# Writing out the counted loops of four engines in a gated cross-attention and mixture-of-experts kernel

## The chip, the core and the metric

The kernel runs on one core of a Trainium2 chip. The core has five engines that run their own instruction streams and meet only through semaphores: TensorE (PE in the profile; PEld is its weight load), VectorE (DVE), ScalarE (ACT), GpSimd (POOL) and SyncE (SP, here only DMA issues). The metric is the device time of one execution in microseconds; less is better.

## What is computed

```
x = x + tanh(g_xattn) * LN(rs * (softmax(q k^T / 4 + mask) v) Wo^T ...)   # 32 x 56 queries, 32 x 1500 context rows, 16 heads of 16
x = x + tanh(g_ffn)   * sum_e w_tok[:, e] * (relu(LN(x) w_fc[e])^2 w_proj[e])   # 8 experts, the two best of each token
```

q comes from the layer-normed x, k and v from the context (`ctx_2048`, 32 x 1500 x 256). All matrices are float32. The kernel keeps their accuracy by splitting each operand into a high and a low part and adding three products (high x high, high x low, low x high).

## The kernel before

**Attention stage.** The 32 batch entries are taken as 16 pairs (`NP`). A pair has 6 groups q of 500 context positions (`PG`), and a group 4 chunks of 125 positions, so a pair has 24 chunks c. TensorE projects k and v of the *next* group while it works on the scores of this one. Its order in a group is: `pv` of the four chunks of the group before, `kv_part(half 0, part 0)`, `scores(c)`, `kv_part(half 0, part 1)`, `scores(c+1)`, `scores(c+2)`, `kv_part(half 1, part 0)`, one of five side tasks (`beside_scores`; none in group 4), `scores(c+3)`, `kv_part(half 1, part 1)`.

Everything that leaves PSUM is shared out by hand. ScalarE takes `exps` (exp of a chunk's scores, L663), `k_hi_evac` (L649), `ctx_high` (L656) and most DMA issues. VectorE clips the probabilities (`clip`, L971), adds the bias of v (`v_evac_step`, L834), takes the low part of k (`k_lo_evac`, L819) and of the context (`ctx_low`, L825), and does the layer norms, sums and divisions in `before_clips`. GpSimd does `inv_std`, `x_plus_beta` and the low part of the expert weights (`expert_lo`).

Two rings matter here. `v_ps` is one PSUM bank: `kv_part(n, half, s, 0)` waits for `v_evac` of the half before it (L413), which VectorE does after the clip of chunk c, which waits for the exp of chunk c. And `pv` waits for `clip_done` of its chunk (L465).

**Expert stage.** 7 blocks f of 256 tokens (`NF`) by 8 experts e. In a step TensorE does `fc(f, e)` and, two steps behind, `proj(f, e - 2)`; between them lie ScalarE's relu (L770), VectorE's square (L1104), ScalarE's high part (L775) and GpSimd's low part (L354). VectorE adds the result to `acc` (L1094).

**Loops.** All the code of an engine is one Python function that calls a helper for a pair or a block. TensorE's pairs are written out already. Pairs 1 to 14 of ScalarE, VectorE and GpSimd, and blocks f from 2 (GpSimd: from 1) of the experts, stand in a `Fori`: one copy of the body with the counter in a register. There every address that depends on the pair, and every semaphore count to wait for, is computed by the engine's sequencer with register instructions (REGISTER_ALU, ISA in the listings; ALU_OP, FUSED_REGOPS, MOVE in the trace). Pair 0 and pair 15 have their constants in the instructions, as have blocks 0 and 1 of the experts. So the same work occurs in one trace in both forms. SyncE has a loop of its own for the loads of the context (L289).

Of the kernel before, what the change touches and what calls it, by code (L numbers as in the profile page):

```python
# [25 lines left out]
NP = B // 2  # L26
# [9 lines left out]
NF = TOK // FT  # L36
# [17 lines left out]
def gated_cross_attention_moe(nc, a, x1_dram, out):  # L54
# [5 lines left out]
    with ExitStack() as ctx:  # L60
# [6 lines left out]
        def plain(ap):  # L67
            return ap.bitcast(fp32)
# [6 lines left out]
        def step(f, e):  # L75

            return f * NE + e if isinstance(f, int) else None
# [231 lines left out]
        @block.gpsimd  # L309
        def _(pool):  # L310
            pool.memset(mhalf[:, :], -0.5).then_inc(ones_done, 1)
            pool.memset(vst[:, :, :, :, HD:VW], 1.0).then_inc(ones_done, 1)
            pool.wait_ge(ones_done, 2)

            def inv_std(ln, i):

                pool.wait_ge(var_done[ln], i + 1)
                pool.tensor_tensor(rstd[ln][0:PW, :], var_e[ln][0:PW, :], mhalf[0:PW, :], ALU.pow)\  # L318
                    .then_inc(rstd_done[ln], 1)

            def x_plus_beta(i):
                pool.wait_ge(xr_in, 16 * i + 16)
                pool.tensor_tensor(xr[0:PW, :], xr[0:PW, :], bet[0:PW, :], ALU.add).then_inc(xb_done, 1)

            def expert_lo(i):

                pool.wait_ge(wehi_done, i + 1)
                pool.tensor_tensor(we_lo[:, bass.ds(i, 1), :, :].squeeze(1), w_raw[:, :, :],
                                   plain(we_hi[:, bass.ds(i, 1), :, :].squeeze(1)), ALU.subtract).then_inc(welo_done, 1)

            def pair(i, first=False, final=False):

                expert_lo(i)
                if not final:
                    inv_std(0, i + 1)
                if not first:
                    x_plus_beta(i - 1)
                    inv_std(1, i - 1)
                    inv_std(2, i - 1)

            inv_std(0, 0)
            pool.wait_ge(scale_done, 4)
            pair(0, first=True)
            with pool.Fori(1, NP - 1) as i:
                pair(i)
            pair(NP - 1, final=True)

            def h_low(f):

                for e in range(NE):  # L350
                    u = f * NE + e
                    at = step(f, e)
                    pool.wait_ge(hhi_done, u + 1)
                    pool.tensor_tensor(h_lo[:, e % NB, :, :], h_sq[:, e % 2, :, :], plain(h_hi[:, e % NB, :, :]),  # L354
                                       ALU.subtract).then_inc(hlo_done, 1)
                    if at == 5:
                        x_plus_beta(NP - 1)
                        inv_std(1, NP - 1)
                    if at == 6:
                        inv_std(2, NP - 1)  # L360

            h_low(0)
            with pool.Fori(1, NF) as f:
                h_low(f)


# [1 line left out]
        def _(pe):  # L368
# [121 lines left out]
            def spread_sums(i):  # L490

                pe.wait_ge(sum_split, 4 * i + 4)
                pe.matmul(side_ps[:, 0:ST * PW], sumsel_r[:, :], sum_hi[:, :, :], start=True, stop=False)  # L493
                pe.matmul(side_ps[:, 0:ST * PW], sumsel_r[:, :], sum_lo[:, :, :], start=False, stop=True).then_inc(sum_done, 1)

            def out_proj(i):
                pe.wait_ge(packed, 16 * ST * (i + 1))
                for k in range(KD):
                    last = pe.matmul(side_ps[0:PW, 0:D], rec[:, 2 * k, :], wo[:, k, :], start=(k == 0), stop=(k == KD - 1))  # L499
                last.then_inc(op_done, 1)  # L500
# [84 lines left out]
            def fc(f, e):  # L585

                u = f * NE + e
                wait(pe, relu_done, u - 1)
                for m in range(KD):
                    ws = slice(m * P, (m + 1) * P)  # L590
                    for k in range(KD):
                        last = mm3(sc_ps[:, e % 2, m * FT:(m + 1) * FT], we_hi[:, 2 * e, k, ws], we_lo[:, 2 * e, k, ws],
                                   yT_hi[:, k, bass.ds(f * FT, FT)], yT_lo[:, k, bass.ds(f * FT, FT)], k == 0, k == KD - 1)
                last.then_inc(fc_done, 1)

            def proj(f, e):

                u = f * NE + e
                pe.wait_ge(hlo_done, u + 1)
                wait(pe, acc_done, 2 * u - 2)  # L600
                for t in range(2):
                    ts = slice(t * P, (t + 1) * P)
                    for k in range(KD):
                        last = mm3(sc_ps[:, 2 + e % 2, t * D:(t + 1) * D], h_hi[:, e % NB, k, ts], h_lo[:, e % NB, k, ts],
                                   we_hi[:, 2 * e + 1, k, :], we_lo[:, 2 * e + 1, k, :], k == 0, k == KD - 1)
                last.then_inc(y2_done, 1)

            def experts(f, first=False):
                for e in range(NE):
                    at = step(f, e)  # L610
                    if not (first and e == 0):
                        fc(f, e)
                    if at == 1:
                        pe.wait_ge(ylo_done, NP)
                        spread_sums(NP - 1)
                    if e >= 2:
                        proj(f, e - 2)
                    elif not first:
                        proj(f - 1, NE - 2 + e)
                    if at == 5:  # L620
                        out_proj(NP - 1)
                    if at == 9:
                        y_transpose(NP - 1)
                    if at == 12:
                        pe.wait_ge(ylo_done, NP + 1)
                        for t in range(RT, NT):
                            router(1, t)
# [4 lines left out]
            for d in range(GC, 0, -1):  # L632
                pv(NP - 1, PC - d)
            experts(0, first=True)
            experts(1)
            with pe.Fori(2, NF) as f:
                experts(f)
            proj(NF - 1, NE - 2)
            proj(NF - 1, NE - 1)
# [3 lines left out]
        def _(act):  # L643
# [112 lines left out]
                k_hi_evac(0, m, 0)  # L756
            act.wait_ge(m_ready, 1)
            pair(0, first=True)
            with act.Fori(1, NP - 1) as i:
                pair(i)  # L760
            pair(NP - 1, final=True)

            def hidden(f, first=False):
                for e in range(NE):
                    u = f * NE + e
                    at = step(f, e)
                    act.wait_ge(fc_done, u + 1)
                    if not (first and e < 2):
                        act.wait_ge(sq_done, u - 1)
                    act.activation(h_relu[:, e % 2, :, :], sc_ps[:, e % 2, :].rearrange("p (m n) -> p m n", m=KD),  # L770
                                   ACT.Relu).then_inc(relu_done, 1)
                    act.wait_ge(sq_done, u + 1)
                    if not (first and e < NB):
                        act.wait_ge(y2_done, u - NB + 1)
                    act.activation(h_hi[:, e % NB, :, :], h_sq[:, e % 2, :, :], ACT.Copy).then_inc(hhi_done, 1)  # L775
                    if at == 0:
                        sums_spread(NP - 1)
                    if at == 7:
                        store_x1(NP - 1)
                    if at == 9:  # L780
                        y_transposed(NP - 1)
                    if at == 15:
                        second_of_two(1)

            hidden(0, first=True)
            hidden(1)
            with act.Fori(2, NF) as f:
                hidden(f)
            act.wait_ge(x1_out, 16 * NP)

# [2 lines left out]
        def _(dve):  # L793
# [284 lines left out]
            dve.tensor_tensor(wr_2[:, :, 1, :], wr[:, :, :], plain(wr_2[:, :, 0, :]), ALU.subtract).then_inc(wr_split, 1)  # L1078
            dve.wait_ge(scale_done, 4)
            pair(0, first=True)  # L1080
            with dve.Fori(1, NP - 1) as i:
                pair(i)
            pair(NP - 1, final=True)

# [12 lines left out]
            def experts(f, first=False):  # L1097
                for e in range(NE):
                    u = f * NE + e
                    dve.wait_ge(relu_done, u + 1)  # L1100
                    if not (first and e < 2):
                        dve.wait_ge(hlo_done, u - 1)
                    r = h_relu[:, e % 2, :, :]
                    dve.tensor_tensor(h_sq[:, e % 2, :, :], r, r, ALU.mult).then_inc(sq_done, 1)  # L1104
                    if e >= 2:
                        accumulate(f, e - 2)
                    elif not first:
                        accumulate(f - 1, NE - 2 + e)
                    beside_experts(step(f, e))
# [31 lines left out]
                    dve.wait_ge(acc_in[2], 16)  # L1141

            experts(0, first=True)
            experts(1)
            with dve.Fori(2, NF) as f:
                experts(f)
            accumulate(NF - 1, NE - 2)
            accumulate(NF - 1, NE - 1)
# [48 lines left out]
```

## Time and profile before

| | us |
|---|---|
| three timed runs | 1261.64 (median), 1258.55, 1262.3 |
| the profiled execution, its own time | 1259.26 |
| its span, first to last instruction | 1257.2 |
| PE busy | 1235.6 (98%) |
| DVE busy | 920.3 (73%) |
| ACT busy | 697.3 (55%) |
| POOL busy | 171.1 (14%) |
| attention stage | about 12 to 1085 |
| expert stage | about 1085 to 1254 |

The time of the execution is its span and 2.1 us around it. Matmuls are pipelined and their ends are modelled, so a busy share of 98% on PE tells only that PE is seldom empty for long; a wait of 0.1 us ahead of a matmul is mostly swallowed by the modelled tail of the one before. Such waits show as longer distances between the starts of like matmuls.

### The profile page before, as it was taken

What the parts mean: (1) busy time and instruction counts of PE and PEld (TensorE: products, weight loads), DVE (VectorE), ACT (ScalarE), POOL (GpSimd) and SP (SyncE); (2) the same over time, 40 slices, a digit from 0 to 9 for tenths busy, and PEclk for the clock granted to TensorE, in tenths of its full rate; (3) what the DMA queues carried; (4) which work ended last, traced back from release to release, by engine and by line L of the source; (5) the groups of instructions that cost most, each with busy time, mean ns of one, the idle gap of its engine ahead of it and who ended that gap; (6) DMA issues with size and microseconds to landing.
All of it is one profiled execution on the core that took longest, in us unless ns stands there. A gap on an engine that the chain in (4) does not pass through costs nothing.

```text
span 1257.2 us, 58770 instructions
## 1 busy us (share of the span) xinstructions
PE 1235.6 (98%) x25460; PEld 1175.5 (94%) x25460; DVE 920.3 (73%) x1806; ACT 697.3 (55%) x854; POOL 171.1 (14%) x142
## 2 busy tenths in 40 slices
PE   6999999999999999999999999999999999999998
PEld 6999999999999999999999999999999999899998
DVE  6667777777777877777777777777777776687555
ACT  4565655655565656565655655665656565244443
POOL 0000101010101010010101010101010100154443
PEclk9999999999999999999999999999999999799999
DMA  4121212121212112121212121212121120020000
GB/s 159 43 76 38 71 54 71 53 68 39 69 55 69 56 41 67 53 71 54 71 37 72 53 71 54 71 38 69 53 69 56 54 67 7 18 63 10 17 8 17
DMA packets 29536, 68.65 MB, mean 55 GB/s; under 512 B 6038, under 2 KB 13459, under 8 KB 29331
## 3 DMA queue, kind: packets, MB, share of 16 engines
q1 hardware_dynamic: 20450, 54.61, 14.1%
q10 hardware_dynamic: 8880, 10.75, 2.7%
q8 instruction: 196, 3.21, 1.0%
q14 instruction: 10, 0.07, 0.0%
HBM read 60.77 MB, written 3.67 MB: 51 GB/s over the span
## 4 chain that ended last, share of the span: by engine, by line
PE 94%; issue 2%; DVE 2%; POOL 1%; DMA 0%; ACT 0%; DVEq 0%; POOLq 0%
PE v_ps L428 24%; PE k_ps L431 21%; PE sc_ps L454 21%; PE o_ps L469 12%; PE sc_ps L371 3%; PE sc_ps L372 3%; PE sc_ps L373 3%; PE k_ps L499 1%; PE k_ps L486 1%; POOL h_lo L354 1%; DVE prob L971 1%; PE k_ps L493 1%; PE k_ps L478 0%; PE k_ps L505 0%; DMA xq<-in_x 0%
## 5 line engine op out<-in xcount | busy, mean ns | idle before, releaser
L663 ACT ACTIVATE prob<-sc_ps,m_bias 125x896 f32<-125x896 f32 x384 | 377.1, 1008 | 336.4 <-PE sc_ps L454 335.1
L971 DVE TENSOR_SCALAR prob<-prob 125x896 f32<-125x896 f32 x384 | 237.3, 624 | 205.3 <-ACT prob L663 201.8
L428 PE MATMUL v_ps<-wv_hi,c_hi 64*125 64x256 f32 x1520 | 317.3, 288 | 3.7 <-DVE c_lo L825 2.6
L431 PE MATMUL k_ps<-c_hi,wk_hi 64*128 64x500 f32 x760 | 314.1, 413 | 0.0
L428 PE MATMUL v_ps<-wv_hi,c_lo 64*125 64x256 f32 x1520 | 301.1, 277 | 0.0
L428 PE MATMUL v_ps<-wv_lo,c_hi 64*125 64x256 f32 x1520 | 300.9, 278 | 0.0
L431 PE MATMUL k_ps<-c_lo,wk_hi 64*128 64x500 f32 x760 | 293.2, 386 | 0.0
L431 PE MATMUL k_ps<-c_hi,wk_lo 64*128 64x500 f32 x760 | 292.2, 384 | 0.0
L428 PEld LDWEIGHTS v_ps<-wv_hi,c_hi 64*125 64x125 f32 x1520 | 225.4, 183 | 16.9 <-DVE c_lo L825 2.8
L428 PEld LDWEIGHTS v_ps<-wv_hi,c_lo 64*125 64x125 f32 x1520 | 229.4, 183 | 0.0
L454 PE MATMUL sc_ps<-q_hi,kh 64*125 64x224 f32 x1536 | 229.0, 278 | 0.0
L428 PEld LDWEIGHTS v_ps<-wv_lo,c_hi 64*125 64x125 f32 x1520 | 228.4, 183 | 0.0
L454 PE MATMUL sc_ps<-q_lo,kh 64*125 64x224 f32 x1536 | 222.7, 270 | 0.0
L454 PE MATMUL sc_ps<-q_hi,kl 64*125 64x224 f32 x1536 | 222.4, 269 | 0.0
L454 PEld LDWEIGHTS sc_ps<-q_hi,kh 64*125 64x125 f32 x1536 | 180.1, 185 | 15.8 <-issue 10.0
L469 PE MATMUL o_ps<-prob,vst 125*17 125x56 f32 x12288 | 175.1, 213 | 3.3 <-issue 1.3
L469 PEld LDWEIGHTS o_ps<-prob,vst 125*17 125x17 f32 x12288 | 156.5, 98 | 19.8 <-issue 6.1
L649 ACT ACTIVATE kh<-k_ps,cst 128x500 fp32r<-128x500 f32 x192 | 130.3, 679 | 56.0 <-PE k_ps L431 55.6
L454 PEld LDWEIGHTS sc_ps<-q_hi,kl 64*125 64x125 f32 x1536 | 158.7, 186 | 0.1
L454 PEld LDWEIGHTS sc_ps<-q_lo,kh 64*125 64x125 f32 x1536 | 157.8, 185 | 0.0
L318 POOL TENSOR_TENSOR rstd<-var_e,mhalf 112x1 f32<-112x1 f32 x48 | 66.4, 1384 | 581.3 <-DVE var_e L809 581.3
L431 PEld LDWEIGHTS k_ps<-c_lo,wk_hi 64*128 64x128 f32 x760 | 141.6, 186 | 0.0
(141 smaller groups left out, 2143.4 us busy)
## 6 DMA issues: line engine op xcount, KB each, us to landing
raw<-in_ctxT SPq DMA_DIRECT2D x96, 500.0 KB, 3.5
w_raw<-in_we ACTq DMA_DIRECT2D x16, 256.0 KB, 5.1
xq<-in_x ACTq DMA_DIRECT2D x16, 112.0 KB, 2.0
xr<-in_x ACTq DMA_DIRECT2D x16, 112.0 KB, 4.2
x_scratch<-x ACTq DMA_DIRECT2D x16, 112.0 KB, 1.9
out_y<-acc SPq DMA_DIRECT2D x7, 256.0 KB, 2.0
acc<-x_scratch SPq DMA_DIRECT2D x1, 1280.0 KB, 7.3
rec<-rec SPq DMA_DIRECT2D x64, 14.0 KB, 2.6
```

The source lines that it names most:

```text
L318: pool.tensor_tensor(rstd[ln][0:PW, :], var_e[ln][0:PW, :], mhalf[0:PW, :], ALU.pow)\
L354: pool.tensor_tensor(h_lo[:, e % NB, :, :], h_sq[:, e % 2, :, :], plain(h_hi[:, e % NB, :, :]), ALU.subtract).then_inc(hlo_done, 1)
L371: pe.matmul(ps, w_h, m_h, start=first, stop=False)
L372: pe.matmul(ps, w_h, m_l, start=False, stop=False)
L373: return pe.matmul(ps, w_l, m_h, start=False, stop=last)
L428: v_last = pe.matmul(v_ps[0:TC, j * D:(j + 1) * D], c_s[v_rows, cs], w_m[v_rows, k, :], start=begin and j == 0, stop=end, skip_group_check ...
L431: k_last = pe.matmul(k_ps[:, half, 0:TG], w[k_rows, k, ws], c_m[k_rows, :], start=begin, stop=end)
L454: last = pe.matmul(sc_ps[0:TC, 2 * (c % 2) + r, m * HS * S:(m + 1) * HS * S], k[rows, g % 2, m, cs], q[rows, b, m, :, :], start=term == 0, ...
L469: last = pe.matmul(o_ps[q * 32:q * 32 + VW, col * S:(col + 1) * S], vst[0:TC, c // GC % 2, c % GC, h, :], prob[0:TC, c % PB, at * S:(at + ...
L649: act.activation(kh[:, s, m, :], k_ps[:, m, 0:TG], ACT.Identity, bias=bk[:, m:m + 1]).then_inc(k_hi, 1)
L663: act.activation(prob[0:TC, c % PB, :].rearrange("p (c n) -> p c n", c=2), sc_ps[0:TC, 2 * (c % 2):2 * (c % 2) + 2, 0:NH * S // 2], ACT.Ex ...
L971: dve.tensor_scalar(p, p, EXP_LO, EXP_HI, ALU.max, ALU.min).then_inc(clip_done, 1)
```

## The change

The `Fori` loops of ScalarE, VectorE, GpSimd (pairs) and of all four engines (expert blocks) become Python loops, so that each pair and block has its own instructions. The loop of SyncE stays.

```diff
@@ gpsimd
-            with pool.Fori(1, NP - 1) as i:
+            for i in range(1, NP - 1):
                 pair(i)
-            h_low(0)
-            with pool.Fori(1, NF) as f:
+            for f in range(NF):
                 h_low(f)
@@ tensor
             experts(0, first=True)
-            experts(1)
-            with pe.Fori(2, NF) as f:
+            for f in range(1, NF):
                 experts(f)
@@ scalar
-            with act.Fori(1, NP - 1) as i:
+            for i in range(1, NP - 1):
                 pair(i)
-            hidden(1)
-            with act.Fori(2, NF) as f:
+            for f in range(1, NF):
                 hidden(f)
@@ vector
-            with dve.Fori(1, NP - 1) as i:
+            for i in range(1, NP - 1):
                 pair(i)
-            experts(1)
-            with dve.Fori(2, NF) as f:
+            for f in range(1, NF):
                 experts(f)
```

No engine operation is added, removed or put in another order, and no wait is added. What goes are the register instructions and the branches. The listed instructions of the program rise from 316 to 923 on ScalarE, from 543 to 1808 on VectorE, from 59 to 146 on GpSimd and from 18478 to 19222 matmuls on TensorE (each with its weight load).

ScalarE, a looped pair, around the exps (L663 before, L661 after) and the evacuations of k (L649, L647), before:

```order
L661 REGISTER_ALU
L663 ISA [waits pv_done,scores_done]
L663 ACTIVATE prob<-sc_ps,m_bias 125x896
L646 REGISTER_ALU
L649 ACTIVATE kh<-k_ps,cst 128x500 [waits kproj_done]
L653 ISA
L73 ISA [waits raw_in0]
L656 ACTIVATE c_hi<-raw 128x1000 [waits vproj_done,kproj_done]
```

and after, the same place in pair 1:

```order
L661 ACTIVATE prob<-sc_ps,m_bias 125x896 [waits pv_done,scores_done]
L647 ACTIVATE kh<-k_ps,cst 128x500 [waits kproj_done]
L654 ACTIVATE c_hi<-raw 128x1000 [waits vproj_done,kproj_done,raw_in0]
L661 ACTIVATE prob<-sc_ps,m_bias 125x896 [waits pv_done,scores_done]
L647 ACTIVATE kh<-k_ps,cst 128x500 [waits scores_done,kproj_done]
```

Before, the wait for the scores sits on a register instruction (ISA) ahead of the exp; after, it sits on the exp.

VectorE, a looped pair, half step u = 9, where the residual of the pair before is made (`x_after`, L913 and L917 before, L910 and L914 after), before:

```order
L971 TENSOR_SCALAR prob<-prob 125x896 [waits exp_done]
L813 TENSOR_SCALAR dlt<-dlt,mv,rstd 112x256 [waits rstd_done1]
L913 TENSOR_TENSOR dlt<-dlt,rowv 112x256 [waits x1_step]
L73 REGISTER_ALU [waits xb_done,x1_step]
L917 TENSOR_TENSOR x<-dlt,xr 112x256 [waits x1_out]
L804 BN_STATS st_2<-x 112x6 [waits x1_done]
```

and after:

```order
L968 TENSOR_SCALAR prob<-prob 125x896 [waits exp_done]
L810 TENSOR_SCALAR dlt<-dlt,mv,rstd 112x256 [waits rstd_done1]
L910 TENSOR_TENSOR dlt<-dlt,rowv 112x256 [waits x1_step]
L914 TENSOR_TENSOR x<-dlt,xr 112x256 [waits x1_out,xb_done,x1_step]
L801 BN_STATS st_2<-x 112x6 [waits x1_done]
```

The register instruction that computes the count for `x1_out` only after `x1_step` has come is gone.

VectorE, the way from the second block of the experts into the third, before:

```order
L965 TENSOR_TENSOR w_tok<-pick 128x16 [waits dve_seq]
L1145 UNCONDITIONAL_BRANCH [waits acc_in2,dve_seq]
L1145 ISA
L1102 REGISTER_ALU [waits relu_done]
L1104 TENSOR_TENSOR h_sq<-h_relu 128x512 [waits hlo_done]
```

and after:

```order
L962 TENSOR_TENSOR w_tok<-pick 128x16 [waits dve_seq]
L1101 TENSOR_TENSOR h_sq<-h_relu 128x512 [waits relu_done,hlo_done,acc_in2,dve_seq]
L1091 SCALAR_TENSOR_TENSOR acc<-sc_ps,w_tok,acc 128x256 [waits acc_done,y2_done]
L1091 SCALAR_TENSOR_TENSOR acc<-sc_ps,w_tok,acc 128x256 [waits acc_done]
L1101 TENSOR_TENSOR h_sq<-h_relu 128x512 [waits hlo_done,relu_done]
```

Between the weights of the tokens and the first square of block 2, three sequencer instructions are gone.

## Rows read from the trace of the kernel before

**Rows 1.** The page: busy time, share and instructions of each engine; the instruction queue.

```profile
PE 1235.6 (98%) x25460; PEld 1175.5 (94%) x25460; DVE 920.3 (73%) x1806; ACT 697.3 (55%) x854; POOL 171.1 (14%) x142
...
q8 instruction: 196, 3.21, 1.0%
```

**Rows 2.** Two lines' own instructions: engine (q: sequencer), operation, count, duration min/median/max ns.

```profile
L663 ACTq FUSED_REGOPS  x336: 37/37/43, 86.3 to 1012.6; - x168
...
L759 ACTq COMPARE_BRANCH  x14: 40/45/59, 148.7 to 1014.0; - x14
```

**Rows 3.** Timeline, pair 0 (constants), group 2: start, duration us, engine, line, operation.

```profile
44.12 0.32 PE L454 MATMUL sc_ps<-q_hi,kl 64*125 64x224 f32 x2
...
44.47 1.01 ACT L663 ACTIVATE prob<-sc_ps,m_bias 125x896 f32<-125x896 f32 x1 [2.40 <-PE sc_ps L454]
...
46.05 0.68 DVE L834 TENSOR_TENSOR vst<-v_ps,rowv 125x512 f32<-125x512 f32 x1
...
47.43 0.28 PE L428 MATMUL v_ps<-wv_hi,c_lo 64*125 64x256 f32 x1
```

**Rows 4.** Timeline, pair 4 (loop), the same four instructions of group 2.

```profile
307.38 0.32 PE L454 MATMUL sc_ps<-q_hi,kl 64*125 64x224 f32 x2
...
307.82 1.01 ACT L663 ACTIVATE prob<-sc_ps,m_bias 125x896 f32<-125x896 f32 x1 [2.50 <-PE sc_ps L454]
...
309.41 0.69 DVE L834 TENSOR_TENSOR vst<-v_ps,rowv 125x512 f32<-125x512 f32 x1
...
310.79 0.28 PE L428 MATMUL v_ps<-wv_hi,c_lo 64*125 64x256 f32 x1
```

**Rows 5.** Chain in order of time: blocks of pv, pairs 0, 5 and 15.

```profile
29.64 1.72 PE o_ps L469 x128
40.48 1.70 PE o_ps L469 x128
51.87 1.70 PE o_ps L469 x128
...
348.21 1.70 PE o_ps L469 x128
359.29 1.70 PE o_ps L469 x128
370.20 1.70 PE o_ps L469 x128
381.68 1.70 PE o_ps L469 x128
...
1013.93 1.70 PE o_ps L469 x128
1024.86 1.70 PE o_ps L469 x128
```

**Rows 6.** Timeline, pair 4, half step 9 and the pv block behind it.

```profile
334.83 0.42 DVE L913 TENSOR_TENSOR dlt<-dlt,rowv 112x256 f32<-112x256 f32 x1
335.38 0.43 DVE L917 TENSOR_TENSOR x<-dlt,xr 112x256 f32<-112x256 f32 x1
...
336.82 2.16 PE L469 MATMUL o_ps<-prob,vst 125*17 125x56 f32 x128
```

**Rows 7.** Timeline, pair 15 (constants), the same two VectorE instructions.

```profile
1065.58 0.42 DVE L913 TENSOR_TENSOR dlt<-dlt,rowv 112x256 f32<-112x256 f32 x1
1066.04 0.42 DVE L917 TENSOR_TENSOR x<-dlt,xr 112x256 f32<-112x256 f32 x1
```

**Rows 8.** Timeline, experts: entry into the loop, then two steps inside it.

```profile
1139.48 0.69 DVE L1104 TENSOR_TENSOR h_sq<-h_relu 128x512 f32<-128x512 f32 x1 [0.33 <-DVE w_tok L965]
...
1142.41 0.38 PE L371 MATMUL sc_ps<-we_hi,h_hi 128*128 128x256 f32 x1 [0.41 <-POOL h_lo L354]
...
1174.25 0.60 ACT L770 ACTIVATE h_relu<-sc_ps 128x512 f32<-128x512 f32 x1 [0.88 <-PE sc_ps L373]
...
1177.11 0.60 ACT L770 ACTIVATE h_relu<-sc_ps 128x512 f32<-128x512 f32 x1 [0.88 <-PE sc_ps L373]
```

**Rows 9.** Windows: span, busy us of PE, PEld, DVE, ACT, POOL, granted clock, DMA, GB/s.

```profile
1080.00:1100.00 20.00, 18.06 (x241) 16.96 (x240) 16.24 (x39) 7.15 (x13) 3.87 (x3) 0.80 0.06 18
```

## The prediction, made before the result was known

> **What bounds the kernel now.** I read the page first. PE is busy for 98% of the span, no other engine for more than 73% [rows 1]. So a gain must come out of TensorE's stream: its own instructions don't change, and what can shrink is waits in front of them. The busy share hides these, so I compared the same work in its two forms. Pair 0 and pair 15 have constants in their instructions, pairs 1 to 14 take them from registers.
>
> Second view, the timeline of group 2 in pair 0 and in pair 4. In pair 0 the scores end at 44.12 + 0.32 = 44.44 and the exp starts at 44.47, 0.03 us later [rows 3]. In pair 4 they end at 307.38 + 0.32 = 307.70 and the exp starts at 307.82, 0.12 later [rows 4]. Between them stands the register instruction that waits for the scores and then computes an address, 336 times on this line, 37 ns each [rows 2]; with its hand-over it comes to the 0.09 us. It isn't overlapped, since it waits itself. The delay travels on: from the scores' end to the end of v's evacuation it is 46.73 - 44.44 = 2.29 us in pair 0 and 310.10 - 307.70 = 2.40 in pair 4. And it reaches TensorE: the third product of the next `kv_part`, which waits for that evacuation (L413), starts 47.43 - 44.44 = 2.99 us after the scores in pair 0, 310.79 - 307.70 = 3.09 in pair 4 [rows 3, 4]. So 0.1 us of TensorE's time per group hangs on ScalarE's sequencer: the ring through `v_ps` has no slack left at 2.4 us, and next to none at 2.3.
>
> Third view, the chain that ended last. It shows every block of pv; the distance from one block to the next is one group. These distances are the terms of my sum, since they have all of a group's waits in them.
>
> **The change part by part.**
>
> Group 0 of a pair, with the loop: 359.29 - 348.21 = 11.08 us (pair 5). With constants: 1024.86 - 1013.93 = 10.93 (pair 15) [rows 5]. Saves 0.15. Pair 15 lacks the DMA issue for the next x on ScalarE, so some of the 0.15 may not be the loop's; the low end is the 0.07 of the next group, the high end 0.15. I take 0.15, because the waits ahead of it are of the same kind.
>
> Group 1: 370.20 - 359.29 = 10.91 against 40.48 - 29.64 = 10.84 (pair 0): 0.07. Group 2: 381.68 - 370.20 = 11.48 against 51.87 - 40.48 = 11.39: 0.09 [rows 5]. Pair 0 lacks VectorE's work for the pair before (reciprocals, division), so again the looped pairs could keep a wait that pair 0 has not. Low end 0, high end these values.
>
> Groups 3 and 4 have the same ring and the same register instructions, but no clean counterpart in pair 0 or 15 (no side task there, or the routers near). I take group 2's 0.09 for each, between 0 and 0.15.
>
> Group 5 has a real stall at its head: pv takes 2.16 us in pair 4 [rows 6] where it takes 1.70 elsewhere [rows 5], 0.46 more, because VectorE is behind with `x_after` when the clips are due. Of that backlog the loop makes two pieces. From L913 to L917 it is 335.38 - 334.83 = 0.55 us with the register count [rows 6] and 1066.04 - 1065.58 = 0.46 without [rows 7]: 0.09. And the clip that starts the backlog waits for an exp that comes some 0.09 earlier, of which group 4's term has counted nearly all; I add 0.03. Sum 0.12; low end 0.09, high end the whole 0.46. What is left of the stall, 0.34, is VectorE's own work and stays: that is what is late next.
>
> Per looped pair: 0.15 + 0.07 + 0.09 + 0.09 + 0.09 + 0.12 = 0.61 us, and 14 such pairs give 8.5 us.
>
> The other register instructions (the addresses of ScalarE's DMAs, VectorE's counts read while it is busy, all on GpSimd in the pairs) I cost at nothing: they run beside an engine instruction or in idle time that nobody waits for. The branches too: 40 to 59 ns, once a pair [rows 2], at places where the next instruction is waited for by no one within a microsecond.
>
> Experts, blocks 2 to 6. A step in the loop takes 1177.11 - 1174.25 = 2.86 us [rows 8], and its 24 matmuls follow each other without a gap; relu, square and the two parts have two steps of room. TensorE's own registers and branch don't show in it. Saves 0. The entry into the loop does: VectorE sits 0.33 us between the tokens' weights and the first square, and TensorE then 0.41 for h_lo [rows 8]. Three sequencer instructions go; about 0.3 of the 0.33 is theirs and TensorE gets it. Between 0 and 0.41, I take 0.3. The last step's chain gets under 0.1 shorter, which I leave out.
>
> Sum: 8.5 + 0.3 = 8.8 us. Against the profiled execution, 1259.3 - 8.8 = 1250.5. That execution lies 2.4 below the median of the three timed ones; the mean of all four is 1260.4, and I take that as the base: 1251.6, rounded 1251.5.
>
> **Two rules of the Trainium skill against these rows.** The exp starts 0.09 us later in the loop [rows 3, 4]. The Trainium skill, Advanced Engine Details and Errata, section Sequencer Loop, says that other engine instructions can be read and queued while the sequencer runs a control instruction. By that alone register work would be free and the sum 0; here the control instruction is the one that waits, so nothing behind it can be under way, and the trace decides for 0.09.
>
> A taken branch costs 40 to 59 ns [rows 2]. The Trainium skill, Runtime: NRT & Kernel Launch, section Instruction fetch mechanics, says that a taken branch out of the two loaded pages stalls for a fetch, and that the sequential fetch of 16 KiB blocks is mostly hidden. The first half would make the loops dearer than I have them; no row shows such a stall. By the second half the slower rival below is worth nothing.
>
> **The rivals.**
>
> *More: VectorE catches up.* If the ring, once under 2.3 us, gives back all of the stall at group 5 (0.46 instead of 0.12), a pair saves 0.95 and the time is 1260.4 - 13.3 - 0.3 = 1246.8. For it: the backlog is short. Against it: pair 15, with constants, runs the same VectorE chain in nearly the same time but for the 0.09.
>
> *Less: only where a twin with the same VectorE load exists.* The references for groups 1 and 2 come from a pair with less VectorE work. If those groups and 3 and 4 keep their waits, 14 x (0.15 + 0.12) + 0.3 = 4.1 us remain: 1256.3. Against it: in pair 4's group 2 the 0.1 us can be followed from the exp to TensorE, and VectorE sat idle before the clip.
>
> *Nothing in the pairs.* TensorE's stream is the bound and the starts only shift inside it; the entry's 0.3 is left: 1260.1. For it: 98% busy. Against it: the distances of rows 5, which are TensorE's own.
>
> *Slower: the code has to be fetched.* The instruction queue moves 3.21 MB in 196 packets that take 1.0% of 16 engines, about 0.010 x 16 x 1257 / 196 = 1.03 us each [rows 1]. The change adds 2 x 744 + 607 + 1265 + 87 = 3447 instructions; with some 60 bytes each (3.21 MB over about 54,000 executed) that is 0.2 MB or 13 packets. If an engine ran dry at each, with 1.03 us on the path, that is 13 us against 8.8: 1264.9. It decides from the ninth such stall on. Against it: pair 0 and the first blocks of experts are straight code on all engines, and neither ScalarE nor VectorE shows such a hole.
>
> **How the numbers follow.** Forecast 0.64, more 0.10, less 0.12, nothing 0.08, slower 0.06. A measurement of this kernel can tell about 0.3%, 3.8 us, from no change. Forecast, more and half of less are faster by over that: 0.80. Half of less and nothing: 0.14. Slower: 0.06. The stage change adds an uncertainty of its own: between 1080 and 1100 the mean granted clock is 0.80 [rows 9], so a part of that work ran at 1.2 GHz, and where such stretches fall after everything has moved by 9 us can cost or give 2 us. The range reaches from the fuller gain, 1246, to 1258, past the rival less and its 2 us.
>
> **What would show it.** In the profile after: the exp 0.03 us after the scores in every pair; blocks of pv 10.9, 10.8 and 11.4 us apart in groups 0 to 2 of middle pairs; pv at the head of group 5 near 2.05 us; VectorE's L914 0.46 after L910; no hole ahead of the first square of block 2; steps of experts still 2.86. A pair takes 66.0 us instead of (1014.0 - 148.7) / 13 = 66.6 [rows 2]. I am wrong if the exp starts early and the distances stay (another wait was just behind), or if new idle time of ScalarE or VectorE appears at odd places, once in a few pairs.

## The result and the profile after

The changed kernel takes 1250.47 us (median of four runs, 1249.57 to 1251.06), the kernel before 1260.28 (four runs, 1258.55 to 1262.3). The ratio is 0.992, with a 95% interval of 0.990 to 0.994. The forecast was 1251.5. The profiled execution after took 1249.57, its span is 1247.4 instead of 1257.2.

Where the 9.8 us are, I read first by stage. The windows are cut at the starts of pv blocks: pair 0; pairs 1 to 14; pair 15; behind the last block of pv. Columns: window, us, busy us of PE, PEld, DVE, ACT, POOL, granted clock, DMA share, GB/s. Before:

```profile
29.57:82.15 52.58, 52.49 (x1252) 50.78 (x1250) 35.34 (x65) 31.97 (x37) 2.19 (x2) 1.00 0.20 60
82.15:1013.86 931.71, 928.09 (x21087) 875.59 (x21085) 706.21 (x1387) 549.40 (x644) 88.67 (x70) 1.00 0.20 59
1013.86:1085.28 71.42, 70.25 (x1487) 66.72 (x1485) 48.26 (x98) 36.10 (x43) 4.32 (x4) 0.93 0.08 26
1085.28:1257.20 171.92, 165.68 (x1477) 164.64 (x1476) 113.27 (x218) 68.14 (x115) 74.79 (x59) 0.99 0.07 23
```

After:

```profile
29.64:82.22 52.58, 52.49 (x1252) 50.78 (x1251) 35.35 (x65) 31.98 (x37) 2.19 (x2) 1.00 0.21 61
82.22:1006.83 924.61, 919.39 (x21087) 870.41 (x21085) 707.20 (x1387) 547.04 (x644) 88.52 (x70) 1.00 0.20 60
1006.83:1076.29 69.46, 69.22 (x1485) 65.78 (x1484) 48.20 (x98) 36.06 (x43) 4.32 (x4) 0.94 0.09 26
1076.29:1247.40 171.11, 165.46 (x1477) 163.97 (x1476) 112.93 (x218) 68.16 (x115) 74.58 (x59) 1.00 0.07 24
```

Pair 0 had constants before and didn't change by 0.01 us. Pairs 1 to 14 lose 7.1 us, pair 15 loses 2.0, the rest 0.8. The counts of instructions agree to within two in every window, so all of it is waiting.

Timeline of group 2 in pair 4, the instructions of [rows 3, 4]:

```profile
305.31 0.32 PE L453 MATMUL sc_ps<-q_hi,kl 64*125 64x224 f32 x2
...
305.66 1.01 ACT L661 ACTIVATE prob<-sc_ps,m_bias 125x896 f32<-125x896 f32 x1 [2.39 <-PE sc_ps L453]
...
307.25 0.69 DVE L831 TENSOR_TENSOR vst<-v_ps,rowv 125x512 f32<-125x512 f32 x1
...
308.63 0.27 PE L427 MATMUL v_ps<-wv_hi,c_lo 64*125 64x256 f32 x1
```

The scores end at 305.63. The exp follows after 0.03 us (0.12 in [rows 4]), v's evacuation ends after 2.31 (2.40), the third product of `kv_part` starts after 3.00 (3.09). Pair 4 now runs as pair 0 does.

The chain, blocks of pv of pair 5 and of pair 15, which answer [rows 5]:

```profile
346.06 1.70 PE o_ps L468 x128
...
356.96 1.70 PE o_ps L468 x128
...
367.78 1.70 PE o_ps L468 x128
...
379.17 1.70 PE o_ps L468 x128
```

```profile
1006.90 1.70 PE o_ps L468 x128
...
1017.80 1.70 PE o_ps L468 x128
```

Groups 0, 1 and 2 take 10.90, 10.82 and 11.39 us, where [rows 5] gave 11.08, 10.91 and 11.48. The medians over pairs 1 to 14, before and after, for groups 0 to 5 are 11.08, 10.91, 11.49, 11.48, 10.20, 11.31 and 10.91, 10.82, 11.38, 11.39, 10.11, 11.20.

Half step 9 of pair 4, and the pv block at the head of group 5 in pair 5 ([rows 6]; that of pair 4 has a hole of another kind in it, told below):

```profile
332.49 0.42 DVE L910 TENSOR_TENSOR dlt<-dlt,rowv 112x256 f32<-112x256 f32 x1
332.95 0.43 DVE L914 TENSOR_TENSOR x<-dlt,xr 112x256 f32<-112x256 f32 x1
```

```profile
400.60 2.06 PE L468 MATMUL o_ps<-prob,vst 125*17 125x56 f32 x128
```

L914 starts 0.46 us behind L910 (0.55 before), pv takes 2.06 at the head of group 5 (2.16 before).

Entry into block 2 of the experts ([rows 8]):

```profile
1129.64 0.18 DVE L962 TENSOR_TENSOR w_tok<-pick 128x16 f32<-128x16 f32 x1
...
1129.85 0.69 DVE L1101 TENSOR_TENSOR h_sq<-h_relu 128x512 f32<-128x512 f32 x1
```

The hole of 0.33 us ahead of the square is gone. The relu of block 2's first step and the next one start 3.86 us apart instead of 4.23, and the steps inside blocks 2 to 6 stay at 2.87 us.

What I had not forecast shows in the chain of pair 14. A block of pv is broken after 109 of 128 matmuls, and the wait is "issue": nothing that the profile shows.

```profile
961.99 1.49 PE o_ps L468 x109
963.48 0.65 issue
964.13 0.47 PE o_ps L468 x19
```

And the instruction queues ([rows 1]: 196 packets before):

```profile
q8 instruction: 202, 3.31, 1.1%
q14 instruction: 32, 0.26, 0.1%
```

### The profile page after: what moved, and what is told of

Its sections match the earlier page's. It is cut to its first block, busy times and chain, and to the rows that moved or that the text cites. A ratio compares the mean times of both kernels' runs of the same rounds, so it can differ in the third digit from the quotient of the medians.

```text
span 1247.4 us, 56326 instructions
## 1 busy us (share of the span) xinstructions
PE 1225.7 (98%) x25460; PEld 1168.8 (94%) x25460; DVE 920.7 (74%) x1806; ACT 694.9 (56%) x854; POOL 170.7 (14%) x142
## 3 DMA queue, kind: packets, MB, share of 16 engines
q8 instruction: 202, 3.31, 1.1%
## 4 chain that ended last, share of the span: by engine, by line
PE 97%; DVE 1%; issue 1%; DMA 0%; ACT 0%; POOL 0%; POOLq 0%; DVEq 0%
PE v_ps L427 23%; PE k_ps L430 22%; PE sc_ps L453 21%; PE o_ps L468 13%; PE sc_ps L370 4%; PE sc_ps L371 4%; PE sc_ps L372 4%; PE k_ps L498 1%; PE k_ps L485 1%; PE k_ps L492 1%; PE k_ps L477 0%; PE k_ps L504 0%; DMA xq<-in_x 0%; PE k_ps L512 0%; PE k_ps L493 0%
## 5 line engine op out<-in xcount | busy, mean ns | idle before, releaser
L661 ACT ACTIVATE prob<-sc_ps,m_bias 125x896 f32<-125x896 f32 x384 | 377.1, 1008 | 328.4 <-PE sc_ps L453 328.3
L427 PE MATMUL v_ps<-wv_hi,c_hi 64*125 64x256 f32 x1520 | 312.6, 285 | 3.2 <-DVE c_lo L822 2.6
L430 PE MATMUL k_ps<-c_hi,wk_hi 64*128 64x500 f32 x760 | 309.5, 407 | 0.0
L647 ACT ACTIVATE kh<-k_ps,cst 128x500 fp32r<-128x500 f32 x192 | 130.4, 680 | 67.1 <-PE k_ps L430 67.1
```

What stands on the lines that cost most here:

```text
L427: v_last = pe.matmul(v_ps[0:TC, j * D:(j + 1) * D], c_s[v_rows, cs], w_m[v_rows, k, :], start=begin and j == 0, stop=end, skip_group_check ...
L430: k_last = pe.matmul(k_ps[:, half, 0:TG], w[k_rows, k, ws], c_m[k_rows, :], start=begin, stop=end)
L647: act.activation(kh[:, s, m, :], k_ps[:, m, 0:TG], ACT.Identity, bias=bk[:, m:m + 1]).then_inc(k_hi, 1)
L661: act.activation(prob[0:TC, c % PB, :].rearrange("p (c n) -> p c n", c=2), sc_ps[0:TC, 2 * (c % 2):2 * (c % 2) + 2, 0:NH * S // 2], ACT.Ex ...
```

## The experiments

The text says "holes" for waits on "issue" inside TensorE's stream. To size them I took TensorE's records one by one (weight loads, matmuls, semaphore instructions), numbered them from the first, and looked at every number that is 193 or 194 above a multiple of 256, where the next weight load came over 0.12 us later than usual. Their sum is the column "holes". All but the first two columns of figures are worked out from the profiled executions, one for each kernel, so a difference of 1 or 2 us in holes between two kernels can be chance. The ratio is to the kernel before on the same chip, which took 1259.51 us for the e_ runs, 1259.49 for a_again, b_free, a_shift and x_late, 1259.87 for a_pad, x_pad and b_shift, and 1258.95 for x_two.

| kernel | median us | ratio to before, 95% | span | holes us | pairs 1-14 | pair 15 | behind it |
|---|---|---|---|---|---|---|---|
| before | 1260.28 | | 1257.2 | 4.8 | 931.7 | 71.4 | 171.9 |
| after | 1250.47 | 0.990-0.994 | 1247.4 | 6.7 | 924.6 | 69.5 | 171.1 |
| a_again | 1252.11 | 0.992-0.995 | 1250.3 | 8.3 | 925.2 | 71.1 | 171.5 |
| e_act | 1251.98 | 0.993-0.996 | 1249.6 | 5.7 | 924.5 | 70.8 | 171.6 |
| e_dve | 1258.2 | 0.998-1.001 | 1256.3 | 5.1 | 931.8 | 69.8 | 171.6 |
| e_pairs | 1250.68 | 0.991-0.995 | 1249.2 | 7.6 | 924.7 | 70.5 | 171.6 |
| e_exp | 1258.81 | 0.998-1.001 | 1257.6 | 4.7 | 933.0 | 70.4 | 171.5 |
| b_free | 1253.05 | 0.994-0.996 | 1251.0 | 6.7 | 924.9 | 72.4 | 171.6 |
| a_shift | 1276.82 | 1.012-1.015 | 1275.9 | 28.6 | 947.4 | 69.7 | 171.6 |
| b_shift | 1282.87 | 1.017-1.020 | 1282.5 | 25.5 | 955.5 | 71.3 | 171.6 |
| x_late | 1252.74 | 0.992-0.995 | 1251.4 | 13.3 | 925.5 | 72.3 | 171.2 |
| a_pad | 1255.17 | 0.996-0.999 | 1248.8 | 1.6 | 925.7 | 68.4 | 171.5 |
| x_pad | 1251.3 | 0.992-0.995 | 1250.3 | 1.1 | 926.0 | 69.6 | 171.5 |
| x_two | 1252.19 | 0.993-0.996 | 1249.5 | 8.6 | 925.1 | 70.6 | 171.5 |

### Which engine's loop: e_act, e_dve, e_pairs, e_exp

e_act: the kernel before with this, and nothing else:

```diff
-            with act.Fori(1, NP - 1) as i:
+            for i in range(1, NP - 1):
```

> The kernel before with only ScalarE's pairs 1 to 14 written out. Theory (the wait of the exp and of k's evacuation sits on a register instruction of ScalarE): nearly the whole gain of the pairs comes from here. In the profile the exp starts 0.02 to 0.03 us after the scores instead of 0.12 to 0.20, groups 1 to 4 of middle pairs take 10.82, 11.39, 11.39 and 10.11 us as in the full change, group 0 about 10.93, group 5 about 11.20 (VectorE's register count of x_after still in it). Sum 0.6 us a pair, 8.5 us in all; with holes in blocks of pv, which come and go, 5 to 9 us faster than before. Rival (VectorE's register instructions are the ones in the ring): within 2 us of before, groups as before.

Measured: 1251.98 us. Chain of e_act, pair 5, groups 0 to 2:

```profile
347.77 1.70 PE o_ps L469 x128
...
358.68 1.70 PE o_ps L469 x128
...
369.50 1.70 PE o_ps L469 x128
...
380.88 1.70 PE o_ps L469 x128
```

10.91, 10.82, 11.38: as in the full change. Pairs 1 to 14 take 924.5 us, the full change 924.6. So the gain in the pairs is ScalarE's loop.

e_dve: the same line with `dve`.

> The kernel before with only VectorE's pairs 1 to 14 written out. Theory (ScalarE's): only group 5 gets shorter, by some 0.09 us a pair (the count for x_after), and perhaps group 0 by a few hundredths; 1 to 2 us faster in all, exp still 0.12 to 0.20 us after the scores. Rival (VectorE's): groups 1 to 4 fall by 0.09 each, 6 to 10 us faster.

Measured: 1258.2 us, no difference that can be told. Chain, pair 5:

```profile
348.67 1.70 PE o_ps L469 x128
...
359.74 1.70 PE o_ps L469 x128
...
370.65 1.72 PE o_ps L469 x128
```

11.07 and 10.91, as with all loops. Only group 5 fell, from 11.31 to 11.21 by the median: the count for `x_after`. The rival, VectorE's registers in the ring, falls.

e_pairs: the same line for `act`, `dve` and `pool`.

> The kernel before with the pairs of ScalarE, VectorE and GpSimd written out, the blocks of experts kept in their loops on all four engines. Theory: the gain of the whole change but for 0.3 to 0.5 us at the entry into the experts' loops; undisturbed groups take 10.90, 10.82, 11.38, 11.38, 10.11 and 11.11 us; 7 to 10 us faster. Rival (a good part of the gain is from the experts or from the clock's second low stretch near 1091, which the kernel after doesn't have): 5 us faster or less, and the span between the first expert block and the end is some 2 us longer than in the kernel after.

e_exp: only the blocks of experts, on all four engines.

```diff
             experts(0, first=True)
-            experts(1)
-            with dve.Fori(2, NF) as f:
+            for f in range(1, NF):
                 experts(f)
```

> The kernel before with only the blocks of experts written out on all four engines, the pairs kept in their loops. Theory: groups as before, no hole of 0.33 us ahead of the first square of block 2, steps still 2.86 us; 0.3 to 0.5 us faster, which can't be told from no change. Rival (experts' registers show in the steps, or the stage change's low clock depends on this code): 2 us or more faster.

Measured: e_pairs 1250.68, e_exp 1258.81. Behind the last block of pv, it takes 171.6 us with looped experts (e_act, e_dve, e_pairs, b_free) and 171.1 or 171.2 with written-out ones (after, x_late). Where the clock falls a second time (next paragraph) it is 171.9 (before) against 171.5 (e_exp, a_again, a_pad, x_pad, x_two). So the experts' loops cost 0.3 to 0.5.

The clock: before, it stands at 0.5 (1.2 GHz) from 1074.3 to 1084.5 and again from 1091.4 to 1094.8. The kernel after shows only the first such stretch. The windows of after and of a_again, the same kernel on another chip:

```profile
1084.00:1089.00 5.00, 4.49 (x38) 4.29 (x37) 4.85 (x8) 1.99 (x4) 1.44 (x2) 1.00 0.01 3
```

```profile
1084.00:1089.00 5.00, 4.91 (x27) 4.92 (x28) 3.63 (x6) 2.15 (x4) 0.81 (x1) 0.66 0.01 3
```

The second stretch comes back in a_again, where the part behind the last block of pv takes 0.4 us more than in after. So it isn't the change that takes it away, and it is worth no more than that.

### Which property of the loop: b_free

All loops stay. ScalarE has no register work left between the wait for the scores and the exp. The counts are computed ahead of the last wait, and the exp reads its bias from the mask of the first pair in every pair, so that its address is a constant. The kernel thus leaves out the masks of the other pairs, and its output is another one. The main lines of the edit (`k_hi_evac` has its two waits exchanged in the same way):

```diff
-                act.wait_ge(scores_done, n + 1)
                 wait(act, pv_done, n - PB + 1)
+                act.wait_ge(scores_done, n + 1)
 ...
-                               scale=SCALE, bias=m_bias[0:TC, bass.ds(n, 1)]).then_inc(exp_done, 1)
+                               scale=SCALE, bias=m_bias[0:TC, c:c + 1]).then_inc(exp_done, 1)
```

> The kernel before, all loops kept, with ScalarE's register instructions taken out of the place between a wait and its instruction: the exp's bias is read from columns 0 to 23 of the mask in every pair (so the mask of pairs 1 to 14 is that of the first pair, and the output is not the reference's), and in exps and k_hi_evac the wait with the older count is written first, so that counts are computed ahead of the wait. Theory (what costs is that a register instruction itself waits): the exp starts within 0.05 us of the scores although the loop is there, groups 1 to 4 within 0.03 of the full change, 5 to 9 us faster than before. Rival (the loop costs by its number of sequencer instructions, wherever they stand, or by its branches): less than half of that, 3 us or less.

Measured: 1253.05 us. Pair 4, group 2 of b_free:

```profile
305.62 0.31 PE L454 MATMUL sc_ps<-q_hi,kl 64*125 64x224 f32 x2
...
305.97 1.01 ACT L663 ACTIVATE prob<-sc_ps,m_bias 125x896 f32<-125x896 f32 x1 [2.40 <-PE sc_ps L454]
```

0.04 us from scores to exp, with the loop in place. Pairs 1 to 14 take 924.9 us against 924.6. The exp's register instruction that waited, 336 times in [rows 2], is gone with the constant address. ScalarE's other 1060 of 1396 are still there, among them one ahead of the wait of every looped exp:

```profile
L662 ACTq ALU_OP  x336: 35/35/53, 83.2 to 1004.9; - x168
```

These cost nothing that can be seen. What cost was the one that waited. That an address computed ahead of the wait would be as cheap as such a count is likely by this, but no run tried it.

### The holes: a_again, a_shift, b_shift

a_shift, the kernel after with 96 more instructions at the start of TensorE's code:

```diff
             pe.wait_ge(cst_in, 16)
+            for _ in range(24):
+                pe.matmul(first_side[0:17, 0:56], cst[:, 0:17], cst[:, 0:56], start=True, stop=True)
             x_transpose(0, first_side)
```

> The kernel after with 24 small matrix products ahead of the first transposition on TensorE (96 instructions more, about a microsecond in a stretch where it waits anyway), which moves all later code of TensorE by about 96 instructions. Theory (the odd holes of 0.2 to 0.9 us in blocks of pv are TensorE running out of code: the instruction queue moves 16 KiB about every 256 instructions, and every hole has such a packet that starts 0.4 to 1.4 us before its block): the holes sit in other blocks of pv than in the kernel after, each again with a packet that starts 0.4 to 1.4 us ahead of the block. Undisturbed groups unchanged, time within 3 us of the kernel after. Rival (the holes come from data transfers or from VectorE, tied to a place in the pair): the same blocks as in the kernel after, group 5 of pairs 3, 4, 6, 7 and 8.

a_again is the kernel after, unchanged.

> The kernel after once more, unchanged, on this chip. By the theory of a_shift the holes in the blocks of pv stand at a place in the code, so most come back in the same blocks (group 5 of pairs 3, 4, 6, 7, 8, group 2 of pair 14), within 0.2 us of their size; if they are chance, fewer than half come back. 8 to 11 us faster than before.

Measured: a_again 1252.11, a_shift 1276.82. Some microsecond of added work made the kernel 25 us slower, where I had expected no more than 3. That the holes move was right. But they moved out of pv, not to other blocks of it, and few of the first nine pairs keep their groups undisturbed. a_again is 7.4 us faster than before on its chip, a little less than the 8 to 11 expected, and than the 9.8 of the first measurement. Chain of a_shift, group 4 of pair 4:

```profile
340.72 1.70 PE o_ps L468 x128
342.42 0.31 PE v_ps L427
...
344.12 1.60 issue
345.72 0.80 PE sc_ps L453 x10
```

The holes now stand behind the blocks of pv; here one of 1.60 us. From the records of a_shift and after, at some of the borders (time us; us since the border 256 records earlier, without the hole; distance between the weight loads there; us since the last packet of queue 8 started):

```
a_shift  345.72   2.87   1.97   2.23     in scores
a_shift  352.88   7.15   0.00   5.92     in pv
a_shift  402.70   3.06   0.76   2.70     in scores
a_shift  410.92   8.21   0.00   7.07     in pv
after    474.04   6.29   0.12   2.30     in kv_part
after    478.88   4.84   0.01   3.70     in pv
after    501.09   4.71   0.41   2.32     in pv
```

3.31 MB in 202 packets are 16384 bytes each, and the 51,823 records of TensorE over 202 are 257 to a packet: 64 bytes per instruction, 256 to a packet. In every hole the code behind the border runs 2.2 us or more after the last packet has started. In the kernel after, half of the borders see the next packet start 0.9 to 2.8 us after TensorE has passed them, a quarter earlier, a quarter later. A block of pv runs its 256 instructions in 1.7 us. In the kernel after the border falls inside pv and both sides last about 5 us; in a_shift it falls at pv's head, the next 256 are gone in 2 to 4 us, and 32 of its 33 holes of over 0.3 us (from 30 to 1060 us) stand behind stretches of 1.7 to 4.0 us. A pair has 7 instructions fewer than 12 packets, so the border moves slowly against the groups, and a bad place lasts for ten pairs.

It isn't a threshold. Of the stretches under 4 us, 42 of 54 ended in a hole in a_shift, but only 4 of 30 in the kernel after, where those of 2.4 to 3.2 us in its last pairs mostly passed. And six of 4.3 to 5.2 us ended in one there, where the packet started late. What delays a packet stays open, and with it why short stretches pass in one place and not in another.

a_again has its holes at the same numbers, but only half at the same blocks: group 5 of pairs 6, 7 and 8 again, not group 5 of pairs 3 and 4 and not group 2 of pair 14, and new or larger ones in group 5 of pairs 2, 5, 9, 11 and 14. So the number decides where a hole can be and, as far as the records show, the packet's delay whether it is one. That most come back was wrong.

b_shift, the same 24 products in the kernel before:

> The kernel before with the 24 small products of a_shift at the start of TensorE's stream. Theory (the 25 us of a_shift are a matter of TensorE's own code and its place against 256 instructions, and have nothing to do with the loops that the change removes): 20 to 26 us slower than before, holes at record numbers 193 and 194 modulo 256, in groups 2 to 4 of pairs 1 to 10. Rival (the streams of ScalarE and VectorE, written out, take the fetches' room, and that is what made a_shift slow): less than 10 us slower, since before has 18 packets of the other instruction queue's 8 KiB kind and after 40.

Measured: 1282.87, 23 us slower than before, with 196 and 9 packets on the two queues. So it doesn't need the written-out streams of the other engines. The holes stand at the expected numbers, but mostly in groups 0 to 4 of pairs 0 to 8 and not only in groups 2 to 4.

### Towards a faster kernel: x_late, a_pad, x_pad, x_two

x_late takes the rest of the stall at group 5 away:

```diff
-                if u == 9 and not first:
-                    x_after(i - 1)
-                    x_after_statistics(i - 1)
 ...
                     if half == 0:
                         clip(i, 2 * u + 1)
+                    if u == 9 and not first:
+                        x_after(i - 1)
+                        x_after_statistics(i - 1)
```

> The kernel after with x_after and its statistics moved from ahead of the two clips of half step 9 to behind them (and the last layer norm from ahead of the clips of half step 10 to behind), and ScalarE's store of x1 and its two loads behind the exp of chunk 20. Theory (what is left of the stall at the head of group 5 is VectorE's backlog from x_after): pv's hole of 0.26 us at c = 18 to 19 is gone in every pair, group 5 takes 10.8 to 10.9 us instead of 11.11; 15 x 0.23 = 3.5 us faster than the kernel after, some 13 us faster than before. Rival (the work then is late in the next group, at the clip of chunk 20 or at y's transposition): the hole moves, the time stays within 1 us of the kernel after or gets worse.

Measured: 1252.74 us, against 1252.11 for a_again on the same chip. Chain, group 5 of pair 4:

```profile
334.35 1.70 PE o_ps L468 x128
...
345.18 0.84 PE o_ps L468 x57
```

The stall is gone: pv takes 1.70 us and the group 10.83. But the block now runs through a border at full speed, the holes grow from 8.3 to 13.3 us, most of them in this block, and take it back. The 3.5 us that I expected over the kernel after didn't come, and the rival's number did, though not by its mechanism.

a_pad adds 8 instructions a pair to the kernel after, so that the border stands still:

```diff
                 pe.wait_ge(xT_done, i + 1)
+                for _ in range(2 if i else 0):
+                    pe.matmul(bank[0:17, 0:8], wq[:, 0, 0:17], xnT[:, 0, 0:8], start=True, stop=True)
                 for m in range(KD):
```

> The kernel after with two tiny matrix products (17 x 8) ahead of each q_proj of pairs 1 to 15 on TensorE, 8 instructions a pair. In the kernel after the first instruction of pv moves from pair to pair by 7 instructions against multiples of 256 (the 16 KiB packets of the instruction queue); with the 8 it stands nearly still, where pairs 0 to 2 have it, and there no hole was seen. Theory (holes are late code, and the place of the packet's border in the program decides): the holes at record numbers 193 and 194 modulo 256 go from 6.7 us in the kernel after to under 2.5 us, also at the end of the attention stage, and the time falls by 3 to 5 us less about 1.5 us for the added products: 1245 to 1249 us on a chip where after has 1250.5. Rival (lateness of packets is chance, wherever the border falls): holes of 5 us or more as before, time as after or 1.5 us slower.

x_pad is x_late with the same.

> x_late with the same two tiny products a pair. Theory: the holes of x_late at group 5 (13.3 us of holes in all in its profile) go for the most part, group 5 takes 10.82 us in nearly all pairs, and the gain of x_late shows: 3 us less than a_pad, 1241 to 1246 us, the fastest of all. Rival (x_late's holes have another cause, such as its later store and loads on ScalarE): holes at group 5 stay at 0.4 to 1.0 us in more than half of the pairs and the time stays above 1249 us.

Measured: a_pad 1255.17 (1250.62 to 1258.78, the profiled execution being the fastest), x_pad 1251.3. Both times missed what I expected, 1245 to 1249 and 1241 to 1246. In both profiles the holes fell to 1.6 and 1.1 us, as expected; in that of a_pad no 256 instructions last under 4.0 us. But the two products cost 0.20 us a pair (group 2 takes 11.58 instead of 11.38), 3.0 us in all, twice what I had put, and what made the other executions of a_pad up to 8 us longer is not known: only one was profiled. In x_pad ScalarE's third DMA issue in a row, moved behind the exp, holds k's evacuation:

```profile
142.96 2.19 ACTq L686 DMA_DIRECT2D w_raw<-in_we  x1
145.25 0.68 ACT L649 ACTIVATE kh<-k_ps,cst 128x500 fp32r<-128x500 f32 x1 [2.14 <-PE sc_ps L453]
```

This happens in pairs 1, 7, 10 and 13 (issues of 1.41 to 2.19 us), where group 5 takes 11.7 to 12.5 us instead of 10.83: 5.3 us in all, which is most of the miss. In x_late, with the same order, that issue took 0.47 at most, so the order alone doesn't explain it.

x_two mends both: the issue at half step 8, and 24 + 40 instructions in two places.

```diff
-                        if not final:
-                            load_matrix(i + 1)
 ...
+                    if u == 8 and not final:
+                        load_matrix(i + 1)
 ...
+            for _ in range(6):
+                pe.matmul(first_side[0:17, 0:8], cst[:, 0:17], cst[:, 0:8], start=True, stop=True)
 ...
+                for _ in range(10 if i == 8 else 0):
+                    pe.matmul(bank[0:17, 0:8], wq[:, 0, 0:17], xnT[:, 0, 0:8], start=True, stop=True)
```

> x_late with two repairs. The load of the expert matrix goes from behind the exp of chunk 20 to the head of half step 8 (in x_pad its issue held ScalarE for up to 2.19 us, ahead of k's evacuation, and group 5 took 12.5 us there). And TensorE's code is moved against the multiples of 256 instructions in two places instead of every pair: 6 tiny products (24 instructions) at the start and 10 (40 instructions, about 1 us) ahead of the q_proj in pair 7, so that pv of group 5 begins at record number 40 or more modulo 256 in every pair. Theory: late code falls from 13.3 us in x_late to under 4 us, group 5 takes 10.82 us in at least 11 of 14 pairs, and the time is 1238 to 1245 us, below every kernel so far. Rival (holes move to other groups, or chance sets them): more than 8 us of holes and 1248 us or more.

Measured: 1252.19 us, 8.6 us of holes. Group 5 takes 10.81 or 10.82 in six of 14 pairs, but holes stand in group 4 of pairs 0 to 2, 7 and 8 and group 2 of pair 7 (the border too near pv's head), and in group 5 of pairs 6 and 12 to 14. The expectation missed by 7 us. None of the four beats the kernel after.

## Why the prediction was right, point by point

**Groups 0 to 4.** By the medians: saved 0.17, 0.09, 0.11, 0.09 and 0.09, forecast 0.15, 0.07, 0.09, 0.09 and 0.09. The doubts there (a missing DMA issue in pair 15, less VectorE work in pair 0) were not needed: e_act has all of it. b_free shows the mechanism as written, the register instruction that waits. It also has all the branches and 1060 of ScalarE's register instructions, which the sum had at nothing, and they cost nothing there.

**Group 5.** Forecast 0.12; the median gives 0.11, and the undisturbed pairs 0.19 (11.29 to 11.10). The step was too small here, since the earlier exp counts in full as well as the 0.09 of the register count (undisturbed pairs take 11.20 with ScalarE's loop alone written out, 11.21 with VectorE's alone, 11.10 with both); holes in pairs 3, 4, 6, 7 and 8 of the kernel after hid that.

**The sum of the pairs.** Forecast 8.5. The medians give 0.66 x 14 = 9.2, the windows 7.1. The 2.1 between them are holes, a term that my sum did not have. Holes are there with the loops too (4.8 us before), and a_again and after differ by 1.6 in them, so writing out doesn't make them: b_free, with all its loops, has 6.7 like the kernel after. But the three kernels whose exp starts late have 4.7 to 5.1 us (before, e_dve, e_exp) and the five whose exp starts early 5.7 to 8.3 (after, a_again, e_act, e_pairs, b_free). So some of the gain may go back into holes whenever the groups get shorter. With one profile of each this isn't shown.

**Experts.** Forecast 0.3 of 0.41, measured 0.3 to 0.5.

**Pair 15 and the stage change.** 2.0 us less in pair 15 stand in no term; I had put 2 us of uncertainty on the clock there. About 1.0 of them are two holes of the execution before, at 1047.5 and 1069.8 (0.85 and 0.68 us), against one of 0.5 after, at 1061.6. Pair 15 takes 68.4 to 72.4 us in the runs of the table whatever was changed. So the hit of 1 us on the total is in part two errors that cancel: 2.1 lost to holes in the pairs, a term at nothing in the sum, and 2.0 won in pair 15 by chance. Later runs on other chips gave 7.4 us (a_again) and, with the pairs alone written out, 8.8 (e_pairs).

**The rivals.** "More" falls: group 5 kept its stall. "Less" and "nothing" fall with e_act. "Slower" had a true core and a wrong place. It put the late code on ScalarE and VectorE, which had to be fetched anew; written out (e_pairs) the pairs take 924.7 us, in loops without the waiting register instruction (b_free) 924.9, so that code costs nothing here. It is TensorE, whose code was straight all along, that runs dry, before and after. Its price of 1.03 us each was near the larger holes. I had looked for such holes on ScalarE and VectorE and in pair 0, not in TensorE's stream over the later pairs.

**The rule on code.** In a_shift TensorE waited 28.6 us at the borders of its own sequential code. The Trainium skill, Runtime: NRT & Kernel Launch, section Instruction fetch mechanics, says that crossing a 16 KiB border is mostly hidden. By that the 96 added instructions would be free. The trace agrees with the 16 KiB and the 256 instructions, and with "hidden" for most borders where these last 4 us or more (148 of 158 in the kernel after passed without a hole).

## What to carry to other kernels

A loop on a helper engine costs by the register instruction that carries the wait: put the computing of counts ahead of the last wait, leave no address to compute behind it, and the loop is nearly free (924.9 against 924.6 us here); write it out only where that can't be done. Look for such costs in the distances between like blocks of the bound engine and not in its busy share. Where TensorE issues 256 short instructions within some 4 us, look at where the 16 KiB borders of its code fall before judging an edit, since adding or removing instructions far away can move the time by more than the edit does. Placing the borders by hand paid in none of the three kernels that tried it here.

## What the hardware showed that I had not expected

- 96 more instructions at the start of TensorE's stream: 25 us more in 1250 (a_shift), 23 in 1260 (b_shift).
- The holes in scores, `kv_part` and pv end 2.2 to 3.3 us after a 16 KiB packet starts, at record number 193 or 194 (seldom 195) modulo 256; the longest is 2.3 us, in x_late.
- Two products of 17 x 8 with float32 operands cost TensorE 0.20 us, while 64 products of 17 x 56 in pv take 1.70 us, 0.03 each. Why the small ones are dearer stays open.
- Three DMA issues in a row on ScalarE took 0.33, 0.44 and 2.19 us in x_pad; in the kernel after, where they stand ahead of the exp, the third took at most 0.98, and in x_late, where they stand as in x_pad, 0.47. Why it takes longer stays open.
